# Wk's second and third chunk in seven block products instead of eight, with GpSimd making sums, in a fused attention and mixture-of-experts block

## The chip, the cores and the metric

The kernel runs on one core of a Trainium2 chip. The metric is the device time of one execution in microseconds; lower is better. The engines are TensorE (PE in the rows), VectorE (DVE), ScalarE (ACT), GpSimd (POOL) and SyncE (SP, which issues most DMA transfers). Each works through a queue of its own in order; semaphores tie the queues together.

## The reference

A pre-normalised block on x of 2048 tokens by 512. First linear attention with 32 heads of 64 (inner width 2048), then a mixture of experts (8 experts, 2 per token), each added to its input:

```python
q = relu(proj(Wq)); k = relu(proj(Wk)); v = proj(Wv)      # proj(W) = layernorm(x) @ W, by heads
kv = einsum('bhsd,bhse->bhde', k, v)
normalizer = clip(einsum('bhsd,bhd->bhs', q, k.sum(axis=2)), 1e-06)
x = x + (einsum('bhsd,bhde->bhse', q, kv) / normalizer) @ Wo + bo
x = x + ffn(layernorm(x))                                  # top-2 gates, w1, silu, w2
```

The change touches only how k = relu(xn @ Wk) is formed, for inner columns 512 to 1535, and the order of the work around it.

## The kernel before

**Precision.** Every large product is made of three: an fp32 operand is split into a rounded part (`_hi`, ScalarE, a cast) and the rest (`_lo`, VectorE, a subtraction), and `three` sums hi x hi, hi x lo and lo x hi in PSUM. So every operand that TensorE reads costs one ScalarE and one VectorE operation, 128 x 512 elements in most cases.

**Tiling.** The 2048 tokens are 16 tiles (NT) of 128. Wk's 2048 columns are 4 chunks (NC) of 512 (CW). Chunk 0 runs together with the first layer norm and the transposes that build `xnT`. In each chunk, for each tile n, `project_k` multiplies the tile (4 blocks of 128 rows, `xnT_hi`, `xnT_lo`) with Wk's chunk into one of the two PSUM banks of `pK` (12 matmuls of 512 columns). ScalarE makes `k_hi` (Relu), VectorE `k_lo` (`split_k`) and adds the tile to the key sum `kacc` (`add_k`). `accumulate_at` then multiplies `xn` with k (12 matmuls) into the four banks of `pA`, which over 16 tiles hold xn^T k. All the split tiles are double buffered. TensorE does project(n+1), accumulate(n), and so on.

**Pairs.** A chunk's `pA` is copied to `at` (`put_at`, two banks by ScalarE and two by VectorE) when its 16 tiles are done. While the next chunk runs, `at` is turned into the matrices m of four head pairs, one pair for four tiles: ScalarE casts wv, wo, at and the key sum (`act_operands`, `act_pair`), VectorE subtracts (`dve_pair`), TensorE does `pe_kv` (nine matmuls of 256 columns into `pT`), ScalarE and VectorE form the block diagonal (`act_kv`, `dve_kv`), TensorE does `pe_m` (three matmuls) and the result is split into `m_hi`, `m_lo`. `at_hl` and `ks_hl` are single, `wv_*` and `wo_*` are double. Chunks 1 and 2 are the two rounds of a loop; chunk 3 follows. The pairs of the last chunk run inside the projection of q that follows; for these four GpSimd makes `wv_lo` and `wo_lo` (`pool_operands`) in place of VectorE. Till then GpSimd has nothing to do.

**Wk's blocks.** A chunk of Wk is 4 blocks of 128 rows. `WK_SPLIT` spreads the splitting of chunks 1 to 3 over the tiles of chunk 0. SyncE loads one chunk at a time into `wk_in`, when the blocks before have been split.

The order of the work is written by hand: each engine has its own program, and the order of the calls in it is the order of its queue.

## Time and profile before

| | |
|---|---|
| median of 3 runs | 1012.17 us (1012.1 to 1013.17) |
| the profiled execution, its own time | 1011.67 us |
| span of the profiled execution | 1010.0 us |
| busy: TensorE, VectorE, ScalarE, GpSimd | 996.3, 686.4, 514.0, 259.3 us |
| granted TensorE clock, mean | 0.999 |
| chunks 1 and 2 in the trace | 105.0 to 293.0 us |

A span runs from the first to the last instruction of the profile; the own time is that of the same execution as the metric counts it. Busy shares are shares of the span. Lines such as L1199 are lines of the kernel before; a helper that is called from many places (`lo` at L1199, `three` at L1614 to L1616) has one line for all of them, and the names of the tiles tell them apart.

### The profile page before, as it was taken

Reading aid. Unit: us, or ns where it says so; the run is one execution under the profiler, and the core shown is the slowest. Engines: PE = TensorE matmul, PEld = TensorE weight load, DVE = VectorE, ACT = ScalarE, POOL = GpSimd, SP = SyncE. Lnnn points to the kernel's source line nnn. Section 1 sums busy time; section 2 is a strip of 40 time slices with the busy share of each in tenths; the row PEclk is TensorE's granted clock in tenths of the full one; section 3 lists DMA queues with packets and bytes.
Section 4 is the critical chain, followed back from the end, with each engine's and each line's share of the span. In section 5 each row is a group of like instructions: output and inputs, shape, how many; then the busy total and the mean of one; then the engine's idle time right before and its main releaser. Section 6 shows DMA issues by size and latency. Waiting matters only on the chain.

```text
span 1010.0 us, 17489 instructions
## 1 busy us (share of the span) xinstructions
PE 996.3 (99%) x5029; PEld 840.0 (83%) x5030; DVE 686.4 (68%) x1552; ACT 514.0 (51%) x1324; POOL 259.3 (26%) x413
## 2 busy tenths in 40 slices
PE   8999999999999999999999999999999989999998
PEld 7888888888888888888788888888888879988996
DVE  7888655565666667667877878777887665544544
ACT  4545444454444457755555555555554954343442
POOL 1000000000000002222423233333333645656564
PEclk9999999999999999999999999999999999999999
DMA  7002501000000011343221111111125635555653
GB/s 262 23 21 84 209 27 36 21 21 21 21 22 21 21 63 63 104 173 116 43 53 49 45 42 42 42 42 42 42 73 161 187 119 101 108 102 99 110 107 48
DMA packets 46861, 75.35 MB, mean 75 GB/s; under 512 B 6089, under 2 KB 18554, under 8 KB 46690
## 3 DMA queue, kind: packets, MB, share of 16 engines
q1 hardware_dynamic: 37010, 56.04, 18.0%
q0 software_dynamic: 9808, 18.79, 10.1%
q8 instruction: 21, 0.34, 0.1%
q14 instruction: 22, 0.18, 0.1%
HBM read 53.14 MB, written 23.50 MB: 76 GB/s over the span
## 4 chain that ended last, share of the span: by engine, by line
PE 93%; DVE 3%; ACT 2%; DMA 1%; issue 1%; SPq 0%; POOL 0%; POOLq 0%; DVEq 0%; ACTq 0%
PE pK L1614 16%; PE pK L1616 16%; PE pK L1615 16%; PE pA L1614 6%; PE pA L1616 6%; PE pA L1615 6%; PE pX L1614 6%; PE pX L1616 5%; PE pX L1615 5%; PE pA L1748 3%; PE pT L1958 2%; PE pT L1694 2%; PE pX L1976 1%; PE pA L1882 1%; DVE w_lo L1523 1%; PE pT L1629 1%
## 5 line engine op out<-in xcount | busy, mean ns | idle before, releaser
L965 ACT ACTIVATE qs<-q,nrec 128x64 f32<-128x64 f32 x512 | 129.6, 336 | 88.0 <-DVE nrec L1344 87.9
L586 POOL TENSOR_TENSOR wv_lo<-wv_in,wv_hi 128x512 fp32r<-128x512 f32 x4 | 5.2, 1292 | 403.0 <-ACT wo_hi L886 403.0
L1614 PE MATMUL pA<-k_hi,xn_hi 128*128 128x512 f32 x256 | 101.0, 394 | 0.5 <-DVE k_lo L1219 0.5
L1614 PE MATMUL pK<-wq_hi,xnT_hi 128*128 128x512 f32 x256 | 100.4, 392 | 0.0
L1614 PE MATMUL pK<-wk_hi,xnT_hi 128*128 128x512 f32 (+1 forms) x256 | 100.1, 391 | 0.2 <-DVE xnT_lo L1199 0.2
L1616 PE MATMUL pK<-wq_hi,xnT_lo 128*128 128x512 f32 x256 | 99.9, 390 | 0.0
L1616 PE MATMUL pA<-k_hi,xn_lo 128*128 128x512 f32 x256 | 99.8, 390 | 0.0
L1615 PE MATMUL pK<-wk_lo,xnT_hi 128*128 128x512 f32 (+1 forms) x256 | 99.7, 390 | 0.0
L1615 PE MATMUL pA<-k_lo,xn_hi 128*128 128x512 f32 x256 | 99.7, 389 | 0.0
L1616 PE MATMUL pK<-wk_hi,xnT_lo 128*128 128x512 f32 (+1 forms) x256 | 99.7, 389 | 0.0
L1615 PE MATMUL pK<-wq_lo,xnT_hi 128*128 128x512 f32 x256 | 99.7, 389 | 0.0
L1614 PE MATMUL pX<-m_hi,qsT_hi 128*128 128x512 f32 x240 | 99.0, 413 | 0.0
L1616 PE MATMUL pX<-m_hi,qsT_lo 128*128 128x512 f32 x240 | 94.2, 393 | 0.0
L1615 PE MATMUL pX<-m_lo,qsT_hi 128*128 128x512 f32 x240 | 93.7, 390 | 0.0
L1337 DVE TENSOR_TENSOR qs<-q,ksum 128x512 f32<-128x512 f32 x64 | 51.8, 809 | 55.6 <-ACT q L959 55.6
L710 POOL DMA_INDIRECT out<-y,slot_token x38 | 70.2, 1847 | 65.0 <-DVE y L1580 43.1
L1219 DVE SCALAR_TENSOR_TENSOR k_lo<-pK,k_hi 128x512 fp32r<-128x512 f32 x64 | 44.0, 688 | 56.1 <-ACT k_hi L833 56.1
L827 ACT CAST xn_hi<-xn 128x512 fp32r<-128x512 f32 x64 | 39.8, 622 | 69.3 <-PE pA L1616 69.3
L959 ACT ACTIVATE q<-pK 128x512 f32<-128x512 f32 x64 | 38.2, 597 | 68.2 <-PE pK L1616 68.2
L833 ACT ACTIVATE k_hi<-pK 128x512 fp32r<-128x512 f32 x64 | 38.1, 595 | 66.4 <-PE pK L1616 66.3
L1141 ACT ACTIVATE hT<-pX,b1T 128x128 f32<-128x128 f32 (+1 forms) x117 | 34.1, 363 | 72.0 <-PE pX L1976 72.0
L1199 DVE TENSOR_TENSOR xn_lo<-xn,xn_hi 128x512 fp32r<-128x512 f32 x64 | 44.0, 688 | 27.7 <-ACT xn_hi L827 27.7
(277 smaller groups left out, 2447.7 us busy)
## 6 DMA issues: line engine op xcount, KB each, us to landing
w_in<-in_ffn_w SPq DMA_DIRECT2D x22, 256.0 KB, 3.6
w_in<-in_ffn_w SPq DMA_DIRECT2D x8, 704.0 KB, 7.6
xn<-in_attn_hidden_states SPq DMA_DIRECT2D x16, 256.0 KB, 6.3
wv_in<-in_attn_Wv SPq DMA_DIRECT2D x16, 256.0 KB, 2.8
wo_in<-in_attn_Wo SPq DMA_DIRECT2D x16, 256.0 KB, 3.0
wk_in<-in_attn_Wq SPq DMA_DIRECT2D x4, 1024.0 KB, 5.7
xnT_dram<-xnT SPq DMA_DIRECT2D x4, 1024.0 KB, 11.6
x_in<-in_attn_hidden_states SPq DMA_DIRECT2D x16, 256.0 KB, 2.6
```

The costliest lines, as they stand in the source:

```text
L710: pool.indirect_dma_start(out, bass.IndirectOffsetOnAxis(slot_token[:, i:i + 1].bitcast(U32), 0), rows, None, bounds_check=T - 1, oob_is_e ...
L827: nc.scalar.copy(xn_hi[:, b * D:(b + 1) * D], xn[:, ds(t * D, D)]).then_inc(xn_hi_ready, 1)
L833: nc.scalar.activation(k_hi[:, b * CW:(b + 1) * CW], pK[:, b * 512:(b + 1) * 512], ACT.Relu).then_inc(k_hi_ready, 1)
L959: nc.scalar.activation(q[:, b * CW:(b + 1) * CW], pK[:, b * 512:(b + 1) * 512], ACT.Relu).then_inc(q_ready, 1)
L965: i = nc.scalar.activation(qs[:, s], q[:, s], ACT.Copy, scale=nrec[:, b * HC + h:b * HC + h + 1])
L1141: last = nc.scalar.activation(hT[0:w, b * P:(b + 1) * P], pX[0:w, b * P:(b + 1) * P], ACT.Silu, bias=b1T[0:w, ds(b * E + e, 1)])
L1199: return nc.vector.tensor_tensor(dst, src, f(hi), ALU.subtract)
L1219: nc.vector.scalar_tensor_tensor(out=k_lo[:, s], in0=pK[:, b * 512:(b + 1) * 512], scalar=0.0, in1=f(k_hi[:, s]), op0=ALU.max, op1=ALU.sub ...
L1337: nc.vector.tensor_tensor(qs[:, b * CW:(b + 1) * CW], q[:, b * CW:(b + 1) * CW], ksum[:, c * CW:(c + 1) * CW], ALU.mult).then_inc(qk_ready, 1)
L1614: nc.tensor.matmul(dst, lhs[0], rhs[0], start=start, stop=False)
L1615: nc.tensor.matmul(dst, lhs[0], rhs[1], start=False, stop=False)
L1616: return nc.tensor.matmul(dst, lhs[1], rhs[0], start=False, stop=stop)
```

## The change

Chunks 1 and 2 are no longer projected one behind the other. Two tiles of tokens (rows a, b), halved in the contraction (256 each), and the two chunks make a 2 x 2 by 2 x 2 block product; it is formed with seven products of blocks instead of eight. The parts:

- Wk: units 4 to 7 are chunk 1's blocks, 8 and 9 a half of chunk 2; GpSimd forms four combinations of halves (each 128 x 1024) in place of others: `t_raw`, twice, one in `wk2_in`, one in `wk_in`. A new load brings chunk 2 to `wk2_in` ahead of `load_wk(1)`. One unit is split per tile n = 2 to 13 of chunk 0, two more after it, chunk 3's during the second pass.
- Rows: for each group of two tiles, GpSimd forms four sums of half tiles (128 x 256, `raw_sum`), which ScalarE and VectorE split (`sum_hi`, `sum_lo`), beside one whole tile (`rows_hi`) and one half (`right_hi`).
- First pass (`pe_group`, 8 groups): seven products of 6 matmuls, between them the accumulation of chunk 1's k in halves of 6 matmuls. ScalarE copies the first product to `p1`; VectorE makes seven sums of 128 x 512 per group from the banks of `pK`: two give chunk 1's tiles in bank 1, two give chunk 2's unclipped tiles in `k2_out`, which SyncE stores to `k2_dram` (the last group's stay in place).
- Second pass (8 steps): chunk 2's tiles are loaded back (`load_k2`, four buffers), split (`split_k2`), summed (`add_k2`) and accumulated, two tiles per step. One head pair (0 to 7) is done in each step; for them GpSimd makes `wv_lo` and `wo_lo`. `at2` holds chunk 1's result.
- Chunk 3 is as before. Its first `load_wq` comes later.

The core of the diff:

```diff
+            sp.dma_start(wk2_in[:, :].rearrange("p (f n) -> p f n", f=FB),
+                         Wk[:, 2 * CW:3 * CW].rearrange("(f p) n -> p f n", p=P)).then_inc(s_wk, 16)
+            sp.wait_ge(wk_lo_ready, FB)
+            load_wk(1)
...
+            for g in range(NG - 1):
+                for i in (1, 0):
+                    sp.wait_ge(k2_ready, 2 * g + 2 - i)
+                    sp.dma_start(k2_dram[2 * g + i], k2_out[:, i * CW:(i + 1) * CW]).then_inc(s_k2out, 16)
+
+            def load_k2(i):
+                if i >= 6:
+                    sp.wait_ge(kacc_done, 2 * NT + i - 3)
+                sp.dma_start(k2_in[i % 4][:, :], k2_dram[tile2(i)]).then_inc(s_block[i % 4], 16)
+
+            def next_pair(n):
+                sp.wait_ge(m_put, n - 1)
+                load_pair(n, n % 2)
+
+            sp.wait_ge(prod_done, 7 * NG)
+            sp.wait_ge(s_k2out, 32 * (NG - 1))
+            for i in range(2, 6):
+                load_k2(i)
+            next_pair(2)
+            load_k2(6)
+            load_k2(7)
+            load_wk(3)
+            next_pair(3)
+            for n in range(4, 8):
+                load_k2(2 * n)
+                load_k2(2 * n + 1)
+                next_pair(n)
+            next_pair(8)
+            next_pair(9)
+            sp.wait_ge(wk_lo_ready, 4 * FB + 2 + FB)
+            load_wq(0)
+            next_pair(10)
+            next_pair(11)
...
+            two = lambda a, h: a[:, 2 * h * CW:2 * (h + 1) * CW]
+            pool.wait_ge(s_wk, 32)
+            pool.tensor_tensor(two(t_raw, 0), two(wk2_in, 0), two(wk_in, 0), ALU.subtract).then_inc(t_step, 1)
+            pool.wait_ge(t_step, 1)
+            pool.tensor_tensor(two(t_raw, 1), two(wk2_in, 1), two(t_raw, 0), ALU.subtract).then_inc(t_step, 1)
+            pool.tensor_tensor(two(wk2_in, 0), two(wk2_in, 1), two(wk2_in, 0), ALU.subtract).then_inc(t_step, 1)
+            pool.wait_ge(t_step, 3)
+            pool.wait_ge(wk_lo_ready, 2 * FB)
+            pool.tensor_tensor(two(wk_in, 1), two(t_raw, 1), two(wk_in, 1), ALU.subtract).then_inc(t_step, 1)
+
+            left = lambda t: xnT[:, t * D:t * D + HALF]
+            right = lambda t: xnT[:, t * D + HALF:(t + 1) * D]
+
+            def raw_sum(g, k):
+                if g == 0 and k == 1:
+                    pool.wait_ge(kproj_done, NT)
+                done = 6 * g + {1: -2, 2: 0, 3: 3, 4: 2}[k]
+                if done > 0:
+                    pool.wait_ge(s_lo_ready, done)
+                if k in (2, 4):
+                    pool.wait_ge(s_step, 4 * g + k // 2)
+                out, a, b, op = {1: (s_raw[0], left(2 * g + 1), right(2 * g + 1), ALU.add),
+                                 2: (s_raw[1], s_raw[0][:, :], left(2 * g), ALU.subtract),
+                                 3: (s_raw[0], left(2 * g), left(2 * g + 1), ALU.subtract),
+                                 4: (s_raw[1], right(2 * g), s_raw[1][:, :], ALU.subtract)}[k]
+                pool.tensor_tensor(out[:, :], a, b, op).then_inc(s_step, 1)
+
+            for g in range(NG):
+                for k in range(1, 5):
+                    raw_sum(g, k)
+
+            for n in (*range(NPOOL), *range(NP - 4, NP)):
...
+            def act_group(g):
+                n = NT + 2 * g
+                if g > 0:
+                    split_c(n - 1)
+                right_hi(g)
+                sum_hi(g, 4)
+                if g > 0:
+                    split_xn(n, 2 * g, 0)
+                act.wait_ge(prod_done, 7 * g + 1)
+                nc.scalar.copy(p1[:, :], pK[:, 0:512]).then_inc(p1_ready, 1)
+                if g == 0:
+                    put_at(0)
+                split_c(n)
+                if g + 1 < NG:
+                    rows_hi(g + 1)
+                else:
+                    at_ready(1)
+                    act_operands(0, 0, 32)
+                    act_pair(0, 0)
+                split_xn(n + 1, 2 * g + 1, 1)
+                if g + 1 < NG:
+                    for k in (2, 1, 3):
+                        sum_hi(g + 1, k)
...
+            split_c(2 * NT - 1)
+            for j in range(8):
+                n = 2 * NT + 2 * j
+                split_k2(2 * j)
+                split_xn(n, tile2(2 * j), 0)
+                act_part(j)
+                act_bd(j)
+                if j == 0:
+                    put_at(1)
+                split_k2(2 * j + 1)
+                split_xn(n + 1, tile2(2 * j + 1), 1)
+                act_m(j)
+                if j == 3:
+                    at_ready(2)
+                if j < 7:
+                    act_operands(j + 1, (j + 1) % 2, 32 * ((j + 1) // 2) + 32)
+                    act_pair(j + 1, (j + 1) % 4)
+                if 3 <= j < 7:
+                    split_wk(NT - 7 + j, 4 * FB + j - 1)
+                if j == 6:
+                    act.wait_ge(prod_done, 7 * NG)
+                    for t in range(2):
+                        nc.scalar.copy(xnT_hi[:, t * D:(t + 1) * D], xnT[:, t * D:(t + 1) * D]).then_inc(xnT_hi_ready, 1)
...
+            def dve_group(g):
+                n = NT + 2 * g
+                b0, b1 = pK[:, 0:512], pK[:, 512:1024]
+                if g > 0:
+                    split_c(n - 1)
+                    add_k(1, n - 1, 1)
+                right_lo(g)
+                sum_lo(g, 4)
+                if g > 0:
+                    split_xn(n, 2 * g, 0)
+                dve.wait_ge(prod_done, 7 * g + 2)
+                dve.wait_ge(p1_ready, g + 1)
+                sub(b1, b1, p1[:, :], ALU.add).then_inc(c_added, 1)
+                dve.wait_ge(prod_done, 7 * g + 3)
+                if g > 0:
+                    dve.wait_ge(c_added, 2 * g)
+                sub(v_sum[:, :], b0, p1[:, :], ALU.add).then_inc(sum_ready, 1)
+                split_c(n)
+                add_k(1, n, 1)
+                if g == 0:
+                    put_at(0)
+                if g + 1 < NG:
+                    rows_lo(g + 1)
+                else:
+                    dve_pair(0, 0, 0)
+                dve.wait_ge(prod_done, 7 * g + 4)
+                dve.wait_ge(sum_ready, 3 * g + 1)
+                dve.wait_ge(c_added, 2 * g + 1)
+                sub(p1[:, :], b0, v_sum[:, :], ALU.add).then_inc(sum_ready, 1)
+                split_xn(n + 1, 2 * g + 1, 1)
+                dve.wait_ge(prod_done, 7 * g + 5)
+                dve.wait_ge(sum_ready, 3 * g + 2)
+                sub(v_sum[:, :], b1, v_sum[:, :], ALU.add).then_inc(sum_ready, 1)
+                if g > 0:
+                    dve.wait_ge(s_k2out, 32 * g)
+                sub(k2_out[:, CW:2 * CW], b1, p1[:, :], ALU.add).then_inc(k2_ready, 1)
+                if g + 1 < NG:
+                    sum_lo(g + 1, 2)
+                    sum_lo(g + 1, 1)
+                    sum_lo(g + 1, 3)
+                dve.wait_ge(prod_done, 7 * g + 6)
+                sub(k2_out[:, 0:CW], b0, p1[:, :], ALU.add).then_inc(k2_ready, 1)
+                dve.wait_ge(prod_done, 7 * g + 7)
+                dve.wait_ge(sum_ready, 3 * g + 3)
+                sub(b1, v_sum[:, :], b1).then_inc(c_added, 1)
...
+                split_k2(2 * j)
+                split_xn(n, tile2(2 * j), 0)
+                add_k2(2 * j)
+                dve_kvT(j)
+                dve_bd(j)
+                if j == 0:
+                    put_at(1)
+                split_k2(2 * j + 1)
+                split_xn(n + 1, tile2(2 * j + 1), 1)
+                add_k2(2 * j + 1)
+                dve_m(j)
+                if j < 7:
+                    dve_pair(j + 1, (j + 1) % 4, (j + 1) % 2)
+                if 3 <= j < 7:
+                    split_wk(NT - 7 + j, 4 * FB + j - 1)
+                if j == 6:
+                    for t in range(2):
+                        dve.wait_ge(xnT_hi_ready, NT + t + 1)
+                        lo(xnT_lo[:, t * D:(t + 1) * D], xnT[:, t * D:(t + 1) * D], xnT_hi[:, t * D:(t + 1) * D]).then_inc(xnT_lo_ready, 1)
...
+                if NPOOL <= n < NP - 4:
...
+            def pe_group(g):
+                n = NT + 2 * g
+                pe.wait_ge(s_lo_ready, 6 * g + 1)
+                pe.wait_ge(wk_lo_ready, 4 * FB)
+                if g == 0:
+                    pe.wait_ge(kacc_done, NT - 1)
+                else:
+                    pe.wait_ge(k2_ready, 2 * g)
+                product(0, rows, 0, 4)
+                pe.wait_ge(kacc_done, n)
+                product(1, rows, HALF, 6)
+                pe.wait_ge(s_lo_ready, 6 * g + 2)
+                pe.wait_ge(p1_ready, g + 1)
+                product(0, sums, 0, 12)
+                if g > 0:
+                    accumulate_half(n - 1, 0)
+                pe.wait_ge(s_lo_ready, 6 * g + 3)
+                pe.wait_ge(sum_ready, 3 * g + 1)
+                product(0, rows, D, 10)
+                if g > 0:
+                    accumulate_half(n - 1, 1)
+                pe.wait_ge(s_lo_ready, 6 * g + 4)
+                pe.wait_ge(kacc_done, n + 1)
+                product(1, sums, HALF, 14)
+                if g == 0:
+                    pe.wait_ge(at_act, 1)
+                    pe.wait_ge(at_dve, 1)
+                accumulate_half(n, 0, g == 0)
+                pe.wait_ge(s_lo_ready, 6 * g + 6)
+                pe.wait_ge(sum_ready, 3 * g + 2)
+                product(0, sums, 2 * HALF, 8)
+                if g == 0:
+                    pe.wait_ge(wk_lo_ready, 4 * FB + 2)
+                pe.wait_ge(k2_ready, 2 * g + 1)
+                product(1, rows, D + HALF, 0)
+                accumulate_half(n, 1, g == 0)
+
+            for g in range(NG):
+                pe_group(g)
+            for j in range(8):
+                n = 2 * NT - 1 + 2 * j
+                pe_kv(j, j % 2)
+                accumulate_at(n, n % 2, False, j == 0)
+                pe_m(j, j % 2)
+                if j == 0:
+                    pe.wait_ge(at_act, 2)
+                    pe.wait_ge(at_dve, 2)
+                accumulate_at(n + 1, (n + 1) % 2, j == 0, False)
+            accumulate_at(3 * NT - 1, 1, False, True)
```

## Rows read from the trace of the kernel before

**Rows 1.** The page: span, busy time of the engines, chain by engine.
```profile
span 1010.0 us, 17489 instructions
...
PE 996.3 (99%) x5029; PEld 840.0 (83%) x5030; DVE 686.4 (68%) x1552; ACT 514.0 (51%) x1324; POOL 259.3 (26%) x413
...
PE 93%; DVE 3%; ACT 2%; DMA 1%; issue 1%; SPq 0%; POOL 0%; POOLq 0%; DVEq 0%; ACTq 0%
```

**Rows 2.** Windows: us, busy per engine (count), granted clock, DMA share, GB/s.
```profile
12.00:16.00 4.00, 3.54 (x22) 2.80 (x20) 3.64 (x11) 2.53 (x9) 0.00 (x0) 1.00 1.06 388
105.00:293.00 188.00, 188.00 (x864) 157.00 (x863) 113.23 (x204) 83.64 (x164) 0.00 (x0) 1.00 0.14 49
```

**Rows 3.** Timeline of TensorE: start us, duration us, line, operation.
```profile
96.86 0.39 PE L1614 MATMUL pK<-wk_hi,xnT_hi 128*128 128x512 f32 x1
...
99.58 0.39 PE L1614 MATMUL pA<-k_hi,xn_hi 128*128 128x512 f32 x1
```

**Rows 4.** Timeline of all engines around the kv step of a pair.
```profile
236.32 0.28 PE L1694 MATMUL pT<-at_hl,wv_hi 128*128 128x256 f32 x1
...
236.43 0.28 PE L1694 MATMUL pT<-at_hl,wv_lo 128*128 128x256 f32 x1
...
238.21 0.28 DVE L1285 TENSOR_TENSOR kvT<-pT,part 128x128 f32<-128x128 f32 x1
```

**Rows 5.** Timeline where ScalarE waits for a projection.
```profile
216.37 0.39 PE L1616 MATMUL pK<-wk_hi,xnT_lo 128*128 x1
...
216.80 0.60 ACT L833 ACTIVATE k_hi<-pK 128x512 fp32r<-128x512 f32 x1 [1.32 <-PE pK L1616]
```

**Rows 6.** Timeline of the first pair whose subtractions GpSimd makes.
```profile
389.68 0.61 ACT L886 CAST wo_hi<-wo_in 128x512 fp32r<-128x512 f32 x1
...
390.20 0.61 ACT L889 CAST at_hl<-at 128x512 fp32r<-128x512 f32 x1
...
390.37 1.29 POOL L586 TENSOR_TENSOR wv_lo<-wv_in,wv_hi 128x512 fp32r<-128x512 f32 x1 [1.15 <-ACT wo_hi L886]
...
390.72 0.29 ACT L890 CAST ks_hl<-kacc 128x128 fp32r<-128x128 f32 x1
...
391.05 1.17 DVE L1276 TENSOR_TENSOR at_hl<-at,at_hl 128x512 fp32r<-128x512 f32 x1 [2.06 <-ACT ks_hl L890]
...
391.62 1.74 POOL L587 TENSOR_TENSOR wo_lo<-wo_in,wo_hi 128x512 fp32r<-128x512 f32 x1
...
392.14 1.37 DVE L1199 TENSOR_TENSOR ks_hl<-kacc,ks_hl 128x128 fp32r<-128x128 f32 x1
...
393.66 0.36 PE L1694 MATMUL pT<-at_hl,wv_hi 128*128 128x256 f32 x1 [0.56 <-DVE ks_hl L1199]
...
393.85 0.28 PE L1694 MATMUL pT<-at_hl,wv_lo 128*128 128x256 f32 x1
```

**Rows 7.** Timeline in the first chunk: VectorE and the next projection.
```profile
28.89 0.68 DVE L1199 TENSOR_TENSOR wk_lo<-wk_in,wk_hi 128x512 fp32r<-128x512 f32 x1
...
29.49 0.68 DVE L1199 TENSOR_TENSOR xn_lo<-xn,xn_hi 128x512 fp32r<-128x512 f32 x1
...
30.27 0.69 DVE L1199 TENSOR_TENSOR xnT_lo<-xnT,xnT_hi 128x512 fp32r<-128x512 f32 x1
...
31.47 0.39 PE L1614 MATMUL pK<-wk_hi,xnT_hi 128*128 128x512 f32 x1
```

**Rows 8.** Groups of GpSimd by line and form: busy us, mean ns.
```profile
L587 POOL TENSOR_TENSOR wo_lo<-wo_in,wo_hi 128x512 fp32r<-128x512 f32 x4 | 6.6, 1650 | 0.0
...
L759 POOL TENSOR_TENSOR cmp<-iota_j,small 128x320 f32<-128x320 f32 x1 | 0.8, 751 | 0.0
```

**Rows 9.** Timeline of SyncE's queue: the issue of Wk's second chunk.
```profile
13.09 0.43 SPq L407 DMA_DIRECT2D wk_in<-in_attn_Wk  x1
```

**Rows 10.** DMA issued from 12 to 24 us: size, us to landing.
```profile
wk_in<-in_attn_Wk SPq DMA_DIRECT2D x1, 1024.0 KB, 10.4
```

**Rows 11.** Waits of TensorE, whole span: total us, times, longest us.
```profile
PE pA L1653 <- POOL ident L567: 1.4, 1, 1.4
```

258 lines of the change are left out of this document (194 added, 64 removed).

## The prediction

> **What bounds the kernel now.** I read the page first. TensorE is busy for 99% of the span and is 93% of the chain that ended last [rows 1]. A busy TensorE could still hide waits, so the windows come next: in the stretch that the change rewrites, second and third chunk, 105.0 to 293.0 us, it is busy for 188.0 of 188.0 us at a granted clock of 1.00, VectorE for 113.2 and ScalarE for 83.6 [rows 2]. So whatever leaves TensorE's queue there is gained, and whatever makes TensorE wait is lost, at face value. The rest is timelines, for how long the other engines need between two steps of TensorE.
>
> The units. Twelve matmuls of 512 columns take 99.58 - 96.86 = 2.72 us, 0.2267 each [rows 3]. Six, half a tile's accumulation or one new block product, take 1.36. A head pair's kv step takes 1.07 (nine of 0.12, as from 236.32 to 236.43 [rows 4]), its m step 0.68. A result can be read 0.20 us after the next matmul could start: last matmul at 216.37, its successor's place is 216.60, ScalarE reads at 216.80 [rows 5]. From one engine's end to the other's start I take 0.04 (ScalarE's ks_hl ends 391.01, at_hl starts 391.05); VectorE to TensorE takes 0.15 (ks_hl ends 393.51, matmul 393.66) and the first matmul behind a stall takes 0.07 more [rows 6]. ScalarE's 512 columns last 0.62 but follow each other every 0.52 [rows 6]; VectorE's last 0.68 and follow every 0.60 [rows 7]. For 256 columns I interpolate between 128 and 512: ScalarE 0.40 (0.29, 0.61 [rows 6]), VectorE 0.42 (0.28 [rows 4], 0.68). GpSimd: 0.75 for 320 columns [rows 8] and 1.29 for 512 [rows 6], so some 0.65 for 256.
>
> **What is removed.** The projections of chunks 1 and 2 were 32 x 12 = 384 matmuls. Now 8 groups of two tiles have 7 products of 6, 336. 48 x 0.2267 = **10.9 us saved**. Accumulations, kv and m steps stay as many.
>
> **First pass: 8 groups.** A group on TensorE is 7 products and 4 half accumulations, 11 x 1.36 = 14.96 us. VectorE has 14 operations of 512 columns and 5 of 256, about 10 us at their pitch; ScalarE 5, GpSimd 2.6. Loads fit; the chains decide. I followed each queue through one steady group, with 0 where its first product starts. The tight place is the second product, which needs bank 1 empty. The last product of the group before ends at -1.36; VectorE forms its difference -1.16 to -0.47, ScalarE makes k_hi -0.43 to 0.17, VectorE k_lo 0.20 to 0.89 and the sum of k to 1.49, TensorE may go at 1.64 where it wanted 1.36: 0.28 + 0.07 = 0.35 per group. Just before, VectorE waits for GpSimd's third half sum (0.65) and its rounding by ScalarE, and comes out of that at the very moment (-1.19) when it is needed; each 0.1 us that GpSimd takes longer is 0.1 more per group. All else in the group (p1, the running sums, the stores of k2_out) has 0.4 us or more to spare. Six groups: 2.1 us. The first group has no half accumulations of an earlier tile to cover its sums and carries put_at(0): 0.2 us before product 3 (p1 ends 107.76) and 1.05 before product 4 (v_sum), and the next group's second product comes 1.2 late since the put shifts VectorE. Sum **5.0 us**; range 3 (chains overlap better) to 9 (GpSimd's half sum at 0.95, towards its 1.29 for 512 columns [rows 6]).
>
> **Second pass: 8 steps.** A step is kv, accumulation, m, accumulation: 1.07 + 2.72 + 0.68 + 2.72 = 7.19 us on TensorE, with a pair's whole preparation in it. Before, a pair had four tiles with their projections, 23.5 us (188.0 / 8). In the new order ScalarE can't prepare pair j+1 before it has split the step's second tile, and that waits for a buffer which the step's first accumulation frees. The loop, from the start of kv(j):
> kv and accumulation with the restart 1.15 + 2.72 = 3.87; freed 0.20, 4.07; ScalarE k_hi, xn_hi, m_hi, wv_hi at pitch 0.52, 0.52, 0.49 (it reads PSUM: 0.60 [rows 5] less the same 0.1 of overlap), 0.52 and wo_hi 0.62, 6.74; GpSimd starts wv_lo at 6.78.
> How long from there to the next kv? Rows 6 show this very sequence once, at the pair behind put_at: GpSimd starts wv_lo at 390.37, VectorE's at_hl (0.68 when alone) lasts 1.17, its ks_hl (0.28 alone) 1.37, GpSimd's wo_lo 1.74 for 1.29, and ks_hl ends at 393.51 [rows 6]. The ends interlock: at_hl is through 0.56 after wv_lo's end at 391.66, wo_lo ends 1.14 after at_hl, ks_hl 0.15 after wo_lo. The two engines take turns, each holding the other for a whole instruction. That is 3.14 us, and c_lo_ready comes at 9.92, kv(j+1) at 10.07. TensorE idles **2.9 us per step** (10.07 - 7.19). Were there no turns, ks_hl would end 1.6 sooner (at_hl from 7.5 in 0.60 and 0.28), and the idle time be 1.3; that is the other bound. The change thus takes the two VectorE subtractions off the pair, 1.2 us where they cost nothing, and puts 2.5 us of GpSimd into the loop.
> In step 0 kv(0) is ready early, but VectorE has the last tile of chunk 1 first: bd_lo ends 4.7, m(0) waits 1.1, put_at(1) 0.45, kv(1) 2.3 us. Steps 1 to 6: 6 x 2.9 = 17.4. In step 7 bd_lo is late by three more subtractions, 1.3. SP's loads of pairs come one step ahead; only pair 3, behind the 1 MB of Wk's last chunk, is near its time, and I cost it at nothing (up to 2). Sum **22.5 us**, with the low bound 3.9 - 1.6 + 6 x 1.3 + 1 = 11.
>
> **Chunk 0.** The load of wk2_in stands ahead of load_wk(1), which was issued at 13.09 [rows 9] and landed 10.4 us later [rows 10]; a second MB on a busy queue moves that by 2.8 us (1 MB at the 388 GB/s of this stretch [rows 2]) to some 26.3, still ahead of ScalarE's wk_hi, whose wk_lo follows at 28.89 [rows 7]. That costs nothing by itself. But GpSimd then forms differences of 1,024 columns, about 2.5 us each (twice 1.25, the distance of the two in [rows 6]), three in a row from 26.3, a fourth around 47. VectorE does wk_lo, xn_lo and xnT_lo one behind the other at 28.89, 29.49 and 30.27, and the last ends at 30.96 for a projection at 31.47 [rows 7]. Taking turns as above, two of the three wait out a whole GpSimd operation, 5.0 - 0.5 of slack = 4.4 us; the fourth costs 2.5 less 0.5, 2.0. I take **6.0**; bounds 0 (no turns) and 9 (all four waits).
>
> **Sum.** -10.9 + 5.0 + 22.5 + 6.0 = +22.6 us. The profiled execution has a span of 1010.0 [rows 1] and its own time is 1011.67; with the sum 1034.3. The median of the runs shown, 1012.17, is 0.5 above that execution: **1035**, rounded, 2.2% slower. Anything within 0.2% (2 us) of 1012.17 could not be told from no change.
>
> **A rule on GpSimd's port.** The rows show waits of half a microsecond and of 1.1 us. The Trainium skill, SBUF — State Buffer, section Who interferes with whom, says that VectorE with two SBUF inputs and a GpSimd instruction reading SBUF exclude each other for the whole instruction. By that rule a 1,024 column difference holds VectorE up to its full length, which no row here shows, and k_lo of the second pass, now read from SBUF, joins the exposed ones; one SBUF input is not exposed, and the seven sums from PSUM would be safe. It speaks against this change, and by it the sum stays the forecast's, where a rule of free passage would give rival B's.
>
> **Rivals.**
> A, the forecast: turns and loop as above. 0.62; own range 1027 to 1043.
> B, the loop but hardly any turns: 5 + 11 + 0 to 2 - 10.9, 1018 (1014 to 1026). For it: the full pattern stands once in rows 6, by chance of timing. Against it: GpSimd's wo_lo takes 1.65 on average over the four pairs of the last quarter [rows 8], so turns are common, and here the order is the one of 390.37 in every step. 0.20.
> C, faster: the pair's operands are ready when kv asks, since ScalarE's queue runs further ahead than I have it. Then no idle time in the second pass but step 0's 2; with 3 in the first and none in chunk 0, 1006. It decides below 0.8 us of idle time per step, where B has 1.3. For it: ScalarE is busy only 6 of 10 us of a step. 0.08.
> D, same, C with chunk 0's cost in full: 0.04.
> E, the clock: the granted clock is 1.00 in every window, although the longest idle stretch of TensorE was only 1.4 us [rows 11], half of what I forecast. If it fell to the lower of its levels, 1.2 GHz, matmuls would take twice as long: seven steps with 14.4 us of TensorE's work where 10.1 were, up to 30 us more, 1065. No row has the lower level. 0.06.
> The Trainium skill, TensorE: Matmul & The Clock Gate, section HAM oscillation — how this bites in real kernels, says that idle gaps of TensorE in every round can put its clock to half each time. By it E would be the outcome if the gaps are long enough.
> Slower 0.62 + 0.20 + 0.06 = 0.88, same 0.04, faster 0.08. The range 1017 to 1044 leaves out C, D, E and the edges of A and B.
>
> **What the profile after would show.** Right: TensorE's matmuls in the rewritten stretch fewer by 48; idle time before the kv matmuls of 2.5 to 3 us, seven times, released by VectorE's ks_hl; k steps of 10 us; ks_hl far above 0.28 us on average; before the groups' second product some 0.35 us, released by the k sum; wk_lo, xn_lo or xnT_lo in chunk 0 beyond 2 us. Wrong: ks_hl at 0.3 and kv idle below 1.3 (B), no idle time at kv (C), a granted clock below 1 (E), or a wait for a load of wv_in or k2_in, whose queue I took to be in time.

## The result, and the profile after

The change made the kernel slower: 1040.82 us (median of 4 runs, 1039.66 to 1042.73) against 1012.13 us (4 runs, 1011.99 to 1013.17), ratio 1.028, 95% interval 1.026 to 1.030. The forecast was 1035, with a range of 1017 to 1044.

The page of the kernel after, in its lines that answer to [rows 1]:
```profile
span 1038.0 us, 17405 instructions
PE 996.8 (96%) x4981; PEld 833.4 (80%) x4982; DVE 727.5 (70%) x1614; ACT 518.4 (50%) x1354; POOL 314.9 (30%) x465
PE 75%; DVE 9%; issue 7%; ACT 5%; POOL 2%; DMA 1%; ACTq 0%; POOLq 0%; DVEq 0%
```
TensorE has the 48 matmuls less that were promised (4,981 for 5,029), though it is busy for as long as before, in part because some of its matmuls ran at half clock, below. In the chain that ended last, TensorE falls from 93% to 75%, and VectorE, ScalarE, GpSimd and the time between instructions (issue) take its place: it waits for the others. For whom, the waits of TensorE over the whole span say (total us, times, longest us):
```profile
PE pT L2007 <- DVE ks_hl L1394: 18.8, 8, 2.7
PE pK L1925 <- DVE xnT_lo L1394: 3.9, 2, 2.5
PE pK L1925 <- DVE kacc L1424: 2.0, 7, 0.8
...
PE pX L1925 <- DVE bd_lo L1394: 1.8, 2, 1.0
...
PE pK L1925 <- DVE v_sum L1434: 0.9, 1, 0.9
```
Three places: before the kv matmuls of the second pass (ks_hl), in chunk 0 (xnT_lo), and in the first pass (kacc, v_sum). An idle time counts here from the modelled end of a matmul, so each stall costs some 0.24 to 0.31 us more in TensorE's pitch (the time from one start to the next). Of the eight waits for ks_hl, seven (18.2 us) lie in the second pass; the eighth, of 0.6, is the one of [rows 6].

I cut the span at three marks of TensorE's timeline: the first product of the first pass, the first kv matmul of the second pass, the first projection of chunk 3. Before, the two outer marks stood at 105.02 and 293.34 us. After, the three stand at 111.79, 234.81 and 321.29. So chunk 0 grew by 6.8; the first pass takes 123.0 where TensorE's 86 blocks of six matmuls (products and half accumulations) at 1.36 are 117.0, 6.1 of stalls; the second takes 86.5 where its matmuls are 60.2, 26.2 more; and behind the third mark both kernels take 716.7. Less the 10.9 saved, and less 0.2 of stalls that this stretch had before, that is +28.0, the difference of the spans.

One step of the second pass, in the timeline of the kernel after; compare the sequence with [rows 6]:
```profile
285.82 0.62 ACT L1031 CAST wo_hi<-wo_in 128x512 fp32r<-128x512 f32 x1
...
286.52 1.28 POOL L657 TENSOR_TENSOR wv_lo<-wv_in,wv_hi 128x512 fp32r<-128x512 f32 x1 [7.20 <-ACT wo_hi L1031]
...
287.20 1.16 DVE L1557 TENSOR_TENSOR at_hl<-at,at_hl 128x512 fp32r<-128x512 f32 x1 [0.26 <-ACT ks_hl L1035]
...
287.76 1.72 POOL L658 TENSOR_TENSOR wo_lo<-wo_in,wo_hi 128x512 fp32r<-128x512 f32 x1
...
288.28 1.35 DVE L1394 TENSOR_TENSOR ks_hl<-kacc,ks_hl 128x128 fp32r<-128x128 f32 x1
...
289.77 0.36 PE L2007 MATMUL pT<-at_hl,wv_hi 128*128 128x256 f32 x1 [2.64 <-DVE ks_hl L1394]
```
It is the sequence of 390.37 again, instruction by instruction. ks_hl, 0.28 alone, needs 1.35: it begins during GpSimd's wo_lo and ends 0.15 after it, in all seven steps of this pass (1.34 to 1.35). e1 below shows that this is the cause. The undisturbed steps take 10.14 us (forecast 10.15).

Chunk 0, VectorE and GpSimd, where before VectorE's three operations took 0.68 each [rows 7]:
```profile
25.92 2.40 POOL L662 TENSOR_TENSOR t_raw<-wk_in 128x1024 f32<-128x1024 f32 x1 [22.32 <-DMA wk_in<-in_attn_Wk]
...
27.20 1.40 DVE L1383 TENSOR_SCALAR xn<-xn,mv,rs 128x512 f32<-128x512 f32 x1
...
28.39 2.46 POOL L664 TENSOR_TENSOR t_raw<-wk_in,t_raw 128x1024 f32<-128x1024 f32 x1
28.52 0.68 DVE L1414 SCALAR_TENSOR_TENSOR k_lo<-pK,k_hi 128x512 fp32r<-128x512 f32 x1
...
29.72 1.68 DVE L1394 TENSOR_TENSOR wk_lo<-wk_in,wk_hi 128x512 fp32r<-128x512 f32 x1
...
30.80 2.81 POOL L665 TENSOR_TENSOR wk_in<-wk_in 128x1024 f32<-128x1024 f32 x1
...
31.32 2.85 DVE L1394 TENSOR_TENSOR xn_lo<-xn,xn_hi 128x512 fp32r<-128x512 f32 x1
...
52.59 2.70 POOL L668 TENSOR_TENSOR wk_in<-t_raw,wk_in 128x1024 f32<-128x1024 f32 x1 [18.97 <-DVE wk_lo L1394]
...
53.12 2.71 DVE L1394 TENSOR_TENSOR xnT_lo<-xnT,xnT_hi 128x512 fp32r<-128x512 f32 x1
```
VectorE's k_lo, whose one operand is in PSUM, lies wholly inside a GpSimd operation and keeps its 0.68. wk_lo, xn_lo and the later xnT_lo, with two operands in SBUF, are held, xn_lo and xnT_lo until 0.5 to 0.6 us behind the end of the GpSimd operation beside them. And xn, with one tensor in SBUF, takes 1.40 where it takes 0.55 alone.

Windows of the kernel after (us, busy per engine, granted clock, DMA share, GB/s):
```profile
234.00:320.00 86.00, 65.60 (x300) 52.47 (x299) 65.48 (x114) 46.31 (x102) 20.67 (x14) 0.96 0.35 107
...
36.00:38.00 2.00, 2.00 (x6) 1.59 (x5) 1.84 (x6) 1.50 (x3) 0.00 (x0) 0.50 0.00 0
246.00:250.00 4.00, 3.85 (x16) 3.29 (x17) 2.74 (x8) 0.86 (x3) 0.00 (x0) 0.68 0.26 66
```
In all of [rows 2] the clock was 1.00. Now, apart from the last 2.1 us of the span, where the kernel before has the lower clock too, it falls to 0.50, 1.2 GHz, three times, at 35.8, 247.4 and 257.7, for 3.4 us each time: twice 1.0 to 1.3 us behind the end of an idle stretch of TensorE of 2.2 to 2.5 us, once 0.2 before the end of one of 2.7. Each fall costs 1.4 to 1.6. Two steps of the second pass last 11.7 and 11.6 instead of 10.1, 3.1 together. In chunk 0 it is 1.4, by comparison with e1 (below), which has the same two stalls there and no fall between them, in TensorE's timelines of the kernel after (first two lines) and of e1:
```profile
34.83 0.50 PE L1925 MATMUL pK<-wk_hi,xnT_hi 128*128 128x512 f32 x1 [2.48 <-DVE xnT_lo L1394]
...
55.89 0.50 PE L1925 MATMUL pK<-wk_hi,xnT_hi 128*128 128x512 f32 x1 [1.38 <-DVE xnT_lo L1394]
...
34.82 0.50 PE L1930 MATMUL pK<-wk_hi,xnT_hi 128*128 128x512 f32 x1 [2.50 <-DVE xnT_lo L1399]
...
54.48 0.50 PE L1930 MATMUL pK<-wk_hi,xnT_hi 128*128 128x512 f32 x1 [1.38 <-DVE xnT_lo L1399]
```

### The profile page after: what moved, and what is told of

Same layout as the page of the kernel before. It is cut to its first block, busy times and chain, and to the rows that moved or that the text cites. A ratio compares the mean times of both kernels' runs of the same rounds, so it can differ in the third digit from the quotient of the medians.

```text
span 1038.0 us, 17405 instructions
## 1 busy us (share of the span) xinstructions
PE 996.8 (96%) x4981; PEld 833.4 (80%) x4982; DVE 727.5 (70%) x1614; ACT 518.4 (50%) x1354; POOL 314.9 (30%) x465
## 4 chain that ended last, share of the span: by engine, by line
PE 75%; DVE 9%; issue 7%; ACT 5%; POOL 2%; DMA 1%; ACTq 0%; POOLq 0%; DVEq 0%
PE pK L1925 13%; PE pK L1927 13%; PE pK L1926 13%; PE pX L1925 5%; PE pX L1927 5%; PE pX L1926 5%; PE pA L1925 4%; PE pA L1926 4%; PE pA L1927 4%; PE pA L2129 3%; PE pT L2339 2%; PE pT L2007 2%; POOL s_raw L685 1%; PE pX L2357 1%; DVE ks_hl L1394 1%
## 5 line engine op out<-in xcount | busy, mean ns | idle before, releaser
L1648 DVE TENSOR_TENSOR qs<-q,ksum 128x512 f32<-128x512 f32 x64 | 45.3, 708 | 60.0 <-ACT q L1154 60.0
L812 POOL DMA_INDIRECT out<-y,slot_token x38 | 66.1, 1739 | 69.3 <-DVE y L1891 44.2
L1925 PE MATMUL pK<-wk_hi,xnT_hi 128*128 128x512 f32 x192 | 76.8, 400 | 6.9 <-DVE xnT_lo L1394 3.9
L1926 PE MATMUL pK<-wk_lo,xnT_hi 128*128 128x512 f32 x192 | 75.6, 394 | 0.0
L1927 PE MATMUL pK<-wk_hi,xnT_lo 128*128 128x512 f32 x192 | 75.4, 393 | 0.0
L657 POOL TENSOR_TENSOR wv_lo<-wv_in,wv_hi 128x512 fp32r<-128x512 f32 x12 | 15.4, 1285 | 193.3 <-ACT wo_hi L1031 193.3
L1925 PEld LDWEIGHTS pA<-k_hi,xn_hi 128*128 128x128 f32 x256 | 48.8, 191 | 11.4 <-ACT at L945 0.7
L1927 PEld LDWEIGHTS pA<-k_hi,xn_lo 128*128 128x128 f32 x256 | 48.6, 190 | 10.5
```

Source lines behind the costliest of these rows:

```text
L812: pool.indirect_dma_start(out, bass.IndirectOffsetOnAxis(slot_token[:, i:i + 1].bitcast(U32), 0), rows, None, bounds_check=T - 1, oob_is_e ...
L1648: nc.vector.tensor_tensor(qs[:, b * CW:(b + 1) * CW], q[:, b * CW:(b + 1) * CW], ksum[:, c * CW:(c + 1) * CW], ALU.mult).then_inc(qk_ready, 1)
L1925: nc.tensor.matmul(dst, lhs[0], rhs[0], start=start, stop=False)
L1926: nc.tensor.matmul(dst, lhs[0], rhs[1], start=False, stop=False)
L1927: return nc.tensor.matmul(dst, lhs[1], rhs[0], start=False, stop=stop)
```

## The experiments

Each has its edit against the changed kernel, from e9 on against the experiment before it; before is 1011.75 to 1011.97 in the runs beside them. The theory was the forecast's: VectorE and GpSimd take turns for whole instructions, and the order of the second pass lets TensorE wait for a pair. The rivals were a bound of another kind in the loop (ScalarE's chain, VectorE's own work, the loads), and that the GpSimd work in chunk 0 is innocent.

**e1, the pair without GpSimd's subtractions.**
```
-            for n in (*range(NPOOL), *range(NP - 4, NP)):
+            for n in range(NPOOL):
+                pool.wait_ge(operands_hi, n + 1)
+                b = slice(n % 2 * D, (n % 2 + 1) * D)
+                pool.memset(f(wv_lo[:, b]), 0.0).then_inc(wv_lo_ready, 1)
+                pool.memset(f(wo_lo[:, b]), 0.0).then_inc(wo_lo_ready, 1)
+            for n in range(NP - 4, NP):
                 pool_operands(n)
```


> Edit: in place of the subtractions that make wv_lo and wo_lo of pairs 0 to 7, GpSimd writes zeros (so these eight pairs lose their low parts); everything else is as in the changed kernel. GpSimd then reads nothing from SBUF in the second pass. Theory A (GpSimd and VectorE take turns, 1.6 us of each step's idle time): ks_hl back to 0.28 us, idle time before kv 1.1 to 1.3 us instead of 2.67, steps of 8.6 us instead of 10.14, and the clock does not fall in the second pass any more (3.0 us). 7 x 1.55 + 3.0 = 14 us less than the changed kernel, about 1027. Rival (the order of ScalarE's queue alone sets the idle time): idle time stays at 2.7 us and the time within 2 us of 1041.


Measured 1026.41, ratio 1.014 (1.012 to 1.016). The timeline of VectorE and GpSimd, from one step to the next,
```profile
278.93 0.53 POOL L695 MEMSET wo_lo<- 128x512 f32 x1
279.15 0.69 DVE L1562 TENSOR_TENSOR at_hl<-at,at_hl 128x512 fp32r<-128x512 f32 x1 [0.26 <-ACT ks_hl L1040]
279.76 0.28 DVE L1399 TENSOR_TENSOR ks_hl<-kacc,ks_hl 128x128 fp32r<-128x128 f32 x1
...
287.77 0.69 DVE L1562 TENSOR_TENSOR at_hl<-at,at_hl 128x512 fp32r<-128x512 f32 x1 [0.26 <-ACT ks_hl L1040]
```
and the waits of TensorE:
```profile
PE pT L2012 <- DVE ks_hl L1399: 9.0, 8, 2.1
```
Both operations are back at the length that they have alone, at_hl although GpSimd still writes its zeros for the first 0.3 us of it. A step takes 287.77 - 279.15 = 8.62, and the second pass 75.2 instead of 86.5 (one clock fall where there were two; in chunk 0 none where there was one). So 10.14 - 8.62 = 1.5 us of each step was the turns; the other 8.62 - 7.19 = 1.4 is the loop itself.

**e2, VectorE subtracts.**
```
-NPOOL = 8
+NPOOL = 0
```


> Edit: VectorE makes wv_lo and wo_lo of pairs 0 to 7 again, as in the kernel before; GpSimd only forms the sums. If the turns are the cost as a matter of contention alone, taking GpSimd out gives back 1.5 us a step, 1028. If it is the length of the serial work behind wo_hi that counts, whoever does it: VectorE starts its four subtractions at 7.5 us of the step (0.60, 0.60, 0.60, 0.28), c_lo_ready at 9.6, kv at 9.75 instead of 10.07; idle time 2.3 instead of 2.67, steps of 9.8, 7 x 0.35 = 2.4 us less, about 1038. I expect the second.


Measured 1038.43 (1.026; 1.025 to 1.028), as forecast. TensorE idles 2.22 to 2.27 per undisturbed step, steps of 9.75 (the clock fell in four others): two more VectorE operations of 0.60 in the loop for 1.5 of turns. Giving the subtractions to GpSimd costs about 0.4 us per step more than it takes off VectorE (9.75 against 10.14).

**e3, no differences of Wk.**
```
-            pool.tensor_tensor(two(t_raw, 0), two(wk2_in, 0), two(wk_in, 0), ALU.subtract).then_inc(t_step, 1)
+            pool.nop(nofuse=True).then_inc(t_step, 1)
...
```
(the other three likewise; and the blocks that t_raw held are split from wk2_in)


> Edit: GpSimd's four differences of Wk's halves (128 x 1024) in chunk 0 are left out; the blocks are split from what lies in their place, so k of chunks 1 and 2 is not the reference's. The extra load and the splitting stay. Theory (the differences hold VectorE up, 6.8 us by the position of chunk 1's first product: 105.0 before, 111.8 after): the first product at 105.0 to 105.5, no idle time before xnT_lo's projection, 1034. Rival (the extra megabyte ahead of load_wk or the new spread of the splitting delays chunk 0): the first product stays beyond 109, 1038 or more.


Measured 1032.1 (1029.99 to 1034.16; ratio 1.021, 1.019 to 1.022). The first product stands at 105.16, where before it was 105.02, and the waits for xnT_lo are gone: so nearly all of chunk 0's 6.8 us came from these four instructions, a clock fall that followed them included, and at most 0.14 from the extra load and the splitting. The second pass, in its window, had no clock fall, with the same waits for ks_hl as after (18.8 us in all, seven of the eight in this pass):
```profile
228.00:312.00 84.00, 63.65 (x304) 50.90 (x303) 65.50 (x114) 46.26 (x103) 20.65 (x14) 1.00 0.37 117
```
It takes 83.4 where it took 86.5 with two falls, which is the 3.1 again.

**e4, the pair first.** ScalarE and VectorE prepare pair j+1 ahead of the split of the step's second tile.
```
                 if j == 0:
                     put_at(1)
-                split_k2(2 * j + 1)
-                split_xn(n + 1, tile2(2 * j + 1), 1)
-                act_m(j)
...
                     act_pair(j + 1, (j + 1) % 4)
+                split_k2(2 * j + 1)
+                split_xn(n + 1, tile2(2 * j + 1), 1)
+                act_m(j)
```


> Edit: in the second pass, ScalarE and VectorE prepare pair j+1 directly behind the block diagonal of pair j, ahead of the step's second tile. Nothing is left out. The loop through ScalarE's buffer wait is gone. By my loop (kv, accumulation, buffer, ScalarE's six operations, turns) kv would be ready at 7.0 us and TensorE never wait there; but VectorE would then be late with everything behind the pair: its queue needs kvT, diagonal 1.5, wait for ks_hl 1.4, the turns 2.45, k_lo, xn_lo, sum, m_lo 2.4, k_lo, xn_lo, sum 1.85 = 9.6 us a step. Theory: steps of 9.6 us, idle time moves from kv to pe_m (bd_lo) and the accumulations, 7 x 0.5 less, and the clock may hold: 1034 to 1038. Rival (VectorE keeps up, since its busy share in the second pass is 76%): steps of 7.4 to 8 us, 1022 to 1025.


Measured 1044.93 (1.033; 1.031 to 1.035): a miss, slower than the change itself. What the theory named did come: the idle time moved from kv to m, and the first two steps take 9.9 and 9.5. From the third on they take 10.8 to 13.4. The waits of TensorE over the second pass,
```profile
PE pX L1925 <- DVE bd_lo L1394: 13.0, 7, 3.3
PE pT L2007 <- DVE ks_hl L1394: 9.3, 6, 4.2
```
ScalarE's waits from 244 to 325 us,
```profile
ACT wv_hi L1030 <- DMA wo_in<-in_attn_Wo: 8.3, 5, 4.0
```
and the timeline of SyncE's queue say where the part beyond the theory comes from:
```profile
257.98 11.35 SPq L496 DMA_DIRECT2D k_in<-k_dram  x2
269.37 0.43 SPq L475 DMA_DIRECT2D wv_in<-in_attn_Wv  x1
```
ScalarE, asking earlier, now meets a pair that isn't loaded. Its load stands in SyncE's queue behind the loads of two k tiles, and they wait for their buffers, 11.35 us from the start of the first to the end of the second. A buffer comes free with VectorE's sum of k, which this edit had itself put behind the pair. The 8.3 us of ScalarE's waits are about what the time exceeds the forecast of 1034 to 1038 by; no run takes them away alone. The forecast of the change had costed these loads at nothing; that held only as long as the rest was late.

**e5, the differences in quarters.** Each of the four becomes four instructions of 256 columns.
```
+            def quarters(out, a, b):
+                for i in range(4):
+                    s = slice(i * HALF, (i + 1) * HALF)
+                    last = pool.tensor_tensor(out[:, s], a[:, s], b[:, s], ALU.subtract)
+                last.then_inc(t_step, 1)
```


> Edit: each of GpSimd's four differences of Wk's halves is made in four instructions of 256 columns instead of one of 1,024; the work is the same. If VectorE waits for the GpSimd instruction that runs, its wait is now 0.65 us at most, not 2.5: chunk 1's first product comes at 106 to 107 us instead of 111.8 (110.0 without the clock's fall), idle time before the projections below 1 us, the clock does not fall there, 1041 - 5 = 1036. If GpSimd's total time counts, the sum of the waits stays: 109 or later, 1039 or more.


Measured 1035.45 (1.022; 1.021 to 1.024), first product at 106.32 for 111.79. The timeline of VectorE:
```profile
27.34 0.67 DVE L1389 TENSOR_SCALAR xn<-xn,mv,rs 128x512 f32<-128x512 f32 x1
...
29.14 0.72 DVE L1400 TENSOR_TENSOR wk_lo<-wk_in,wk_hi 128x512 fp32r<-128x512 f32 x1
29.78 1.23 DVE L1400 TENSOR_TENSOR xn_lo<-xn,xn_hi 128x512 fp32r<-128x512 f32 x1
30.93 1.22 DVE L1400 TENSOR_TENSOR xnT_lo<-xnT,xnT_hi 128x512 fp32r<-128x512 f32 x1
```
The same differences, in pieces of a quarter of the columns, and no operation of VectorE in chunk 0 is lengthened by more than 0.55 where it was up to 2.2. The turn is taken by the instruction: its length, not GpSimd's total, is the price. The gain in the total is less clear than in chunk 0, since the second pass, which the edit leaves alone, had the clock at 0.50 for 13.7 us in this trace and took 89.4.

**e6, the difference in SBUF.** The fourth result of a group goes to a buffer of its own (c_buf) instead of back into its PSUM bank; TensorE's second product waits for that store, no longer for the relu and the sum of k, which read the buffer.
```
-                sub(b1, v_sum[:, :], b1).then_inc(c_added, 1)
+                sub(c_buf[:, :], v_sum[:, :], b1).then_inc(c_added, 1)
...
-                pe.wait_ge(kacc_done, n)
+                if g == 0:
+                    pe.wait_ge(kacc_done, n)
+                else:
+                    pe.wait_ge(c_added, 2 * g)
```


> Edit: the difference that gives chunk 1's second tile goes to a buffer in SBUF (c_buf, 512 columns) instead of back into PSUM bank 1; its split and key sum read it there, and the next group's second product waits for the difference alone. If the chain difference, k_hi, k_lo, key sum is what holds the second product (seven waits, 2.0 us of idle time and 0.24 us of restart each), all seven vanish: the first pass takes 119.3 to 120 us instead of 123.0, 1041 - 3 = 1038. Rival: VectorE and GpSimd now meet more often (k_lo and the sum read two operands from SBUF), and the time stays within 1 us of the changed kernel or rises.


Measured 1035.65 (1032.5 to 1037; ratio 1.022, 1.021 to 1.024). The first pass takes 119.0 for 123.0 and all seven waits for kacc are gone. The total, forecast at 1038, fell by 2 us more, within the spread that the clock brings. VectorE's operations on the buffer keep their 0.69, so the rival's more frequent turns didn't come.

**e7, the second pass reordered.** VectorE subtracts; ScalarE casts wv and wo ahead of the second tile and at and ks right behind it; kvT stands ahead of the sum of k; and SyncE issues the pair's load between the two k tiles, as e4 taught.
```
+                if j < 7:
+                    act_operands(j + 1, (j + 1) % 2, 32 * ((j + 1) // 2) + 32)
                 if j == 0:
                     put_at(1)
                 split_k2(2 * j + 1)
                 split_xn(n + 1, tile2(2 * j + 1), 1)
-                act_m(j)
...
-                    act_operands(j + 1, (j + 1) % 2, 32 * ((j + 1) // 2) + 32)
                     act_pair(j + 1, (j + 1) % 4)
+                act_m(j)
```


> Edit: second pass alone. VectorE makes wv_lo and wo_lo; both engines handle pair j+1's wv and wo behind the diagonal of pair j, at and ks behind the step's second tile, m last; VectorE forms kvT ahead of the key sum; SyncE issues the load of a pair between the two loads of k tiles, not behind both. By my queues VectorE needs 7.1 to 7.3 us for a step and TensorE 7.19: steps of 7.3 to 7.8 us instead of 10.14, idle time below 0.5 us a step, no fall of the clock: second pass 65 to 68 us instead of 86.5, 1041 - 20 = 1021. Rival 1 (as where the pair was only moved early: loads late): ScalarE waits for wo_in, steps of 9 us or more, 1032. Rival 2 (VectorE's real need is longer, from its share of 76% at 10.14 us, 7.7 us): steps of 8.2, 1026.


Measured 1025.93 (1.014; 1.013 to 1.016), second pass 72.7. The forecast of 1021 was missed, and 1026 is the number that the rival of a busier VectorE gave. No engine waits for a load any more, and the steps take 7.83, 8.43 where a block of Wk is split, for 7.19 of matmuls: a third limit, which I read as VectorE's work (e10 shows that it wasn't). The two ends of the pass stand out too: 2.3 us in step 0, before the accumulation that waits for put_at(1), with a clock fall behind it, and 1.5 before m(7).

**e8, quarters, c_buf and the order together.**


> Edit: the three edits of quarters, c_buffer and reordered together. If the losses are separate places on TensorE's time line, the gains add: 1041 - 5 - 3 - 20 = 1013, and the kernel is within 2 us of the one before. If removing one uncovers another (VectorE's load in the two passes), it stays above 1017. The 10.9 us of removed matmuls can show as a gain only if the rest costs less than that.


Measured 1017.5 (1.005; 1.003 to 1.007). From 1040.82 the three gains, 5.4, 5.2 and 14.9 taken singly, would give 1015.4; together they give 23.3. The forecast was 1013, or above 1017 if one removal uncovers another. By place nearly nothing was uncovered: the first pass takes 119.0 and the second 72.7, as singly, and the first product stands at 107.19 for e5's 106.32. What is missing against the forecast is mostly what e7 had missed. The gains of single runs also hold clock falls that come and go, so they don't add to a microsecond.

**e9, the ends.** On top of e8: put_at(1) ahead of the pair's wv and wo in step 0, the splits of Wk for chunk 3 in steps 4 to 7 and VectorE's part of the split of xnT in step 7.
```
-                if 3 <= j < 7:
-                    split_wk(NT - 7 + j, 4 * FB + j - 1)
+                if j > 3:
+                    split_wk(NT - 8 + j, 4 * FB + j - 2)
```


> Edit on top of the three together: in step 0 of the second pass put_at(1) goes ahead of the next pair's wv and wo on both engines; the splits of Wk's last four blocks move from steps 3 to 6 to steps 4 to 7, and the two xnT_lo of chunk 3 from step 6 to step 7, where no pair is prepared. In the kernel with all three edits the second pass takes 72.7 us for 60.2 us of TensorE's work: 2.3 us idle before the accumulation behind put_at, 1.5 before the last pe_m, 0.6 per split. If these are places of their own: 1.2 + 1.5 + 0.6 us less and no fall of the clock in step 0 (1.7), 1017.5 - 3.5 to 5 = 1012.5 to 1014. If VectorE is the bound from end to end (7.8 us a step), its work is only moved, and it stays above 1016.


Measured 1012.58 (11 runs, 1012.14 to 1013.23), ratio 1.0007 (0.9998 to 1.0016): the time of before. The second pass takes 68.6, and TensorE's clock no longer falls in it.

**e10, the first group.** On top of e9: the last accumulation of chunk 0, 2.7 us of TensorE's work, in halves inside group 0.
```
                 product(0, sums, 0, 12)
-                if g > 0:
-                    accumulate_half(n - 1, 0)
+                accumulate_half(n - 1, 0, False, g == 0)
```


> Edit on top of e9: the last accumulation of chunk 0 is done in two halves inside the first group, as cover for the first group's sums, and put_at(0) comes later. Before, the first group waits 0.21 us for p1 and 0.88 for v_sum (1.6 us with the restarts). Theory: these go, a wait of 0.3 us for put_at(0) comes: 1 to 1.5 us less than e9, 1011 to 1013, that is, not to be told from the kernel before (1012.0). Rival: the first group's queues are too full (two blocks of Wk are split there too), and a longer wait takes their place: e9's time or more.


Measured 1012.24 (11 runs, 1011.75 to 1012.85), ratio 1.0003 (0.9994 to 1.0012): still the time of before. v_sum's stall of 0.9 is gone; a new one of 1.1 stands before an accumulation of the same group. The trace names no engine for it, but the program waits there for put_at(0), and VectorE's part of that ends just before it:
```profile
113.23 1.27 DVE L1445 COPY at<-pA 128x512 f32<-128x512 f32 x2
114.60 0.47 PE L1954 MATMUL pA<-k_hi,xn_hi 128*128 128x512 f32 x1 [1.08 <-issue]
```
In the second pass, VectorE's group wv_lo from 250 to 258 us waits:
```profile
L1409 DVE TENSOR_TENSOR wv_lo<-wv_in,wv_hi 128x512 fp32r<-128x512 f32 x1 | 0.7, 692 | 0.7 <-ACT wo_hi L1039 0.7
```
So the limit of 7.83 that I had read as VectorE's work in e7 was its work and 0.7 of waiting for ScalarE's wo_hi, while ScalarE itself sat idle for 1.03 behind kvT.

**e11, wv_hi and wo_hi ahead of bd_hi.** On top of e10.
```
                 act_part(j)
+                if 0 < j < 7:
+                    act_operands(j + 1, (j + 1) % 2, 32 * ((j + 1) // 2) + 32)
                 act_bd(j)
                 if j == 0:
                     put_at(1)
-                if j < 7:
-                    act_operands(j + 1, (j + 1) % 2, 32 * ((j + 1) // 2) + 32)
+                    act_operands(1, 1, 32)
```


> On top of e10: in steps 1 to 6 of the second pass ScalarE makes wv_hi and wo_hi of the next pair ahead of bd_hi, in the 1.03 us in which it waited for VectorE's kvT. In e10 VectorE then waited 0.71 us per step for wo_hi, and the six steps last 7.83 (7.84 to 8.44 where a block of Wk is split) against 7.19 of TensorE's work. If that wait of VectorE is what holds the loop, as I hold, the steps become 7.2 to 7.3 without a split of Wk and about 7.85 with one, since VectorE's own operations of a step sum to 7.05 and 7.65: together about 3.4 us less, 1009, faster than the kernel before by 0.3%. The rival is that ScalarE's bd_hi, now behind two casts more, comes late, and m with it: 0.1 to 0.5 per step is given back, and the time is 1010.5 to 1012, with idle time of TensorE moved from kv to m, released by bd_lo.


Measured 1008.36 (5 runs, 1007.76 to 1008.52) beside 1011.83, ratio 0.996 (0.995 to 0.998): 0.4% faster than the kernel before, clear of noise though small, and 32 us faster than the change. The page,
```profile
span 1006.8 us, 17400 instructions
...
PE 989.6 (98%) x4981; PEld 830.9 (83%) x4982; DVE 724.1 (72%) x1630; ACT 519.0 (52%) x1354; POOL 295.5 (29%) x461
```
a window over the second pass,
```profile
225.00:290.00 65.00, 62.52 (x301) 50.64 (x300) 62.04 (x127) 45.64 (x102) 0.00 (x0) 1.00 0.45 138
```
and from the timeline of TensorE what is left of its stalls there (two more like the last):
```profile
230.51 0.47 PE L1955 MATMUL pA<-k_hi,xn_hi 128*128 128x512 f32 x1 [0.40 <-ACT at L953]
...
234.67 0.39 PE L2038 MATMUL pT<-at_hl,wv_hi 128*128 128x256 f32 x1 [1.18 <-DVE ks_hl L1410]
...
268.31 0.50 PE L1955 MATMUL pX<-wo_hi,bd_hi 128*128 128x512 f32 x1 [0.23 <-DVE bd_lo L1410]
```
The second pass takes 65.1 for 60.2 of matmuls, at a clock of 1.00. VectorE is busy for 62.0 of 65.0 there, so I think that little more is to be had from order alone; no run tries it.

## Why the prediction was right, and where its sizes were off

Its likeliest case, A, is what happened, in each of its places: 1040.82 lies in A's own range. Against the sum, in order of its terms:

- **Saved, 10.9.** Shown by the count, 48 matmuls fewer, and their pitch. What is left of it depends on the stalls: e11 is faster than before by 3.5, so 7.4 us of stalls still eat the rest, 4.9 of them in the second pass.
- **First pass, forecast 5.0, measured 6.1.** (The terms that the forecast names are 2.1, 0.2, 1.05 and 1.2, 4.6 together; the rest of its 5.0 isn't accounted for.) The waits are where they were put: v_sum 0.88 (forecast 1.05), before the next group's second product 0.83 (1.2), six times 0.20 (0.28), and 0.2 at p1. What was too small is the cost beside the idle time: I had 0.07 for the restart, and with the part that the modelled end hides it is 0.24 to 0.28, nine times; a tenth stall, of 0.3, is hidden nearly whole. e6 shows the cause of seven of them. GpSimd's half sums took 0.74 for the 0.65 of the forecast, and the wait did not grow by it.
- **Second pass, forecast 22.5, measured 26.2.** Idle time per step 2.64 as the trace counts it and 2.95 in the pitch of the steps (10.14 less 7.19), forecast 2.9. The excess is the clock, 3.1, and 0.6 in sum in the steps. The turns are 1.5 of each step by e1 (forecast 1.6) and the loop 1.4 (1.3): both halves of the term are shown. The Trainium skill, SBUF — State Buffer, section Who interferes with whom, gives the whole instruction as the unit of exclusion; e1 and e5 agree (1.35 falls to 0.28 when GpSimd doesn't read, 2.85 to 1.23 with quarters).
- **Chunk 0, forecast 6.0, measured 6.8.** The cause is shown by e3, the unit by e5. That the number is so near is in part luck. The two stalls for xnT_lo are 2.5 and 1.4 long, 4.2 with their restarts, where I had 4.4 and 2.0 (which is 6.4, and I took 6.0). The 4.4 was too much: wk_lo and xn_lo were held for 1.0 and 2.2, not for two whole operations. Two terms that were not in the sum fill the gap: some 1.4 at three transposes of xn, which VectorE also had late, less 0.2 of slack, and 1.4 from a clock fall.
- **SyncE's loads at nothing.** True for the change, where no engine waits for a load in the second pass, but in e4 the same queue makes ScalarE wait for 8.3 us: it is the place where, the clock apart, my model of the loop had a part missing.

**Rival E, the clock**, had been kept apart with 0.06 as up to 30 us. It is real and small: three falls, 3.1 us in the second pass and 1.4 in chunk 0, 4.5 together, in an execution of 1039.74 for which the sum gave 1034.3. So of the signs of being wrong one came, a granted clock below 1, beside those of A. I had treated it as all or nothing, seven whole steps at half clock or none; it strikes some steps, for 3.4 us, and leaves others. With the clock left out, the excess of 1.1 in the first pass and 0.6 in the second and the 0.6 too much in chunk 0 partly cancel. The clock also goes with the spread: the four runs of e3 take 1029.99, 1031.5, 1032.71 and 1034.16 us at mean granted clocks of 0.999, 0.997, 0.996 and 0.994, and those of the change 1039.66 to 1042.73 at 0.994 to 0.991, where those of before spread over 1.2. Rival B fails on ks_hl, 1.35 long in each step, and e1, without turns, shows its time, 1026. C and D fail on the 2.2 to 2.7 us at each kv.

**What stays open.** Why one idle stretch of 2.6 us goes with a clock fall and the next, equal one doesn't. e3 had all seven of the second pass and no fall, the kernel after had two falls in the same pass, e2 with stretches of 1.8 to 2.3 four; no run here separates them.

## What to carry to other kernels

Fewer instructions on the engine that bounds a kernel are worth their full time only if the others can feed it in the time that is left. Here 10.9 us less of TensorE's work made room in which three queues, each with slack before, became late; 39 us of stalls and half clock came in for them, and only shorter GpSimd instructions, a buffer more and a new order of ScalarE's, VectorE's and SyncE's queues brought the saving out, 3.5 us of it.
Work is not free on GpSimd because GpSimd is idle: ask which VectorE instruction that works in SBUF lies beside it, those with both operands there above all, and who waits for that one. Where it has to be there, cut it into short instructions.
When an engine's sum per step is under the pitch of the step, it isn't the bound, however busy: look for the one wait inside it (0.7 us for wo_hi), and for an idle stretch of the engine that it waits for.
